# Score products in twos over two pairs of PSUM banks, and new hand-written orders, in a four-layer batch pipeline on one core

## What is computed

```
# L0: per-batch bottleneck weights from a hypernetwork
down = relu(x @ (Wd + dWd[b]).T + bd);  x = x + down @ (Wu + dWu[b]).T + bu
# L1: layer norm, weight and bias, plus a conditional bias
x = (layernorm(x) * weight + bias + tanh(lin(cond))) * weight + bias
# L2: attention block with conditional scale and shift, 16 heads of 16
h = layernorm(x) * g1 + b1;  q, k, v = split(h @ W_qkv.T + b_qkv)
o = softmax(q @ k.T / 4) @ v;  x = x + (o @ W_o.T + b_o) * a1
h = layernorm(x) * g2 + b2;  x = x + (gelu_tanh(h @ W_f1.T + b_f1) @ W_f2.T + b_f2) * a2
# L3: RMS norm, gated unit with exact gelu, 8-bit rows, ternary weights
h = x * scale(cond) * rsqrt(mean(x*x) + eps);  val, gate = split(h @ up_w.T)
y = quant8(val * gelu(gate)) @ ternary(down_w).T;  out = y + x
```

## Time and profile before

| | before |
|---|---|
| median of 3 runs | 934.47 us |
| span of the profiled execution | 933.9 us |
| PE busy | 843.1 us (90%), 5852 instructions |
| VectorE (DVE) busy | 565.4 us (61%) |
| ScalarE (ACT) busy | 510.9 us (55%) |
| GpSimd (POOL) busy | 231.2 us (25%) |

### The profile page before, as it was taken

One profiled execution on the slowest core, in us unless ns is written; L12 is line 12 of the kernel. 1 busy time (PEld: TensorE's weight loads), 2 busy tenths in 40 slices (PEclk: granted clock), 3 DMA queues, 4 the chain that ended last, 5 costly groups with the idle time before them and its releaser, 6 DMA issues.

```text
span 933.9 us, 15916 instructions
## 1 busy us (share of the span) xinstructions
PE 843.1 (90%) x5852; PEld 633.5 (68%) x5852; DVE 565.4 (61%) x1063; ACT 510.9 (55%) x796; POOL 231.2 (25%) x333
## 2 busy tenths in 40 slices
PE   6642577999999999999999999999999999999977
PEld 4101355687777778787878787878777777776665
DVE  1212586575757667575858585858485867656424
ACT  1101444565565657574748575656666574756542
POOL 1001204150405041323232231405050514130310
PEclk9855777999999999999999999999999999999998
DMA  9997643423161433324151515151424132320000
GB/s 344 365 366 252 248 138 124 148 80 122 62 203 38 135 97 114 120 78 156 47 187 47 188 47 188 46 173 61 154 76 142 65 127 80 104 80 25 24 12 12
DMA packets 58477, 118.48 MB, mean 127 GB/s; under 512 B 6336, under 2 KB 15936, under 8 KB 55696
## 3 DMA queue, kind: packets, MB, share of 16 engines
q1 hardware_dynamic: 58400, 117.48, 36.6%
...
## 4 chain that ended last, share of the span: by engine, by line
PE 74%; issue 9%; DMA 7%; DVE 4%; ACT 2%; SPq 2%; POOL 2%; POOLq 0%; DVEq 0%; ACTq 0%
PE bank L486 30%; PE bank L692 11%; PE pair_s L653 6%; PE pair_s L618 5%; PE pair_t L639 5%; PE pair_t L486 4%; DMA hyp<-in_hyper 3%; PE bank L737 3%; PE bank L664 3%; PE bank L567 2%; PE bank L729 1%; PE bank L561 1%; DVE oq L1145 1%; DMA wc<-in_cols 1%; PE bank L574 1%
## 5 line engine op out<-in xcount | busy, mean ns | idle before, releaser
L851 ACT ACTIVATE Pr<-pair_t 128x1024 f32<-128x1024 f32 x128 | 131.3, 1026 | 125.2 <-PE pair_t L639 121.5
L1121 DVE TENSOR_REDUCE nmax<-pair_s 128x4 f32<-128x1024 f32 x128 | 155.8, 1217 | 34.5 <-PE pair_s L618 33.9
L692 PE MATMUL bank<-wf,G 128*128 128x256 f32 x512 | 123.0, 387 | 0.1
L486 PE MATMUL bank<-wup_hi,hD_hi 128*128 128x512 f32 x256 | 109.4, 427 | 4.8 <-POOL hD_lo L1316 4.1
L1344 POOL TENSOR_TENSOR x<-x,xcr 128x512 f32<-128x512 f32 x16 | 20.5, 1281 | 358.1 <-DVE x L1179 358.1
L692 PEld LDWEIGHTS bank<-wf,G 128*128 128x128 f32 x512 | 93.3, 190 | 15.5 <-issue 0.2
L486 PE MATMUL bank<-wup_lo,hD_hi 128*128 128x512 f32 x256 | 102.0, 398 | 0.0
L486 PE MATMUL bank<-wup_hi,hD_lo 128*128 128x512 f32 x256 | 101.9, 398 | 0.0
L618 PE MATMUL pair_s<-Kp,Qp 64*128 64x256 f32 x512 | 66.1, 337 | 21.7 <-DVE nmax L1121 13.0
L895 ACT ACTIVATE gl<-bank,rsD 128x512 f32<-128x512 f32 x64 | 44.1, 689 | 63.6 <-PE bank L486 63.4
L1189 DVE SCALAR_TENSOR_TENSOR hd<-bank,rsD,gl 128x512 f32<-128x512 f32 x64 | 47.9, 748 | 46.2 <-PE bank L486 34.7
(11 more groups left out here) (177 smaller groups left out, 1879.5 us busy)
## 6 DMA issues: line engine op xcount, KB each, us to landing
hyp<-in_hyper SPq DMA_DIRECT2D x16, 1024.0 KB, 10.2
...
```

The lines of the kernel that those rows point to most:

```text
L486: mm = pe.matmul(dst, l, r, start=first and i == 0, stop=last and i == 2)
L692: mm = pe.matmul(bank[5][:, r * D:(r + 1) * D], G[:, k, r * P:(r + 1) * P], wf2[:, k, :], start=k == 0, stop=k == FT - 1)
L851: act.activation(Pr[:, p % 4, :, :].rearrange("p a n -> p (a n)"), pair_t[:, :, :].rearrange("p a n -> p (a n)"), ACT.Exp, scale=DH ** -0. ...
L1121: dve.tensor_reduce(nmax[:, n % 2, :, p % GP, :], pair_s[:, :, :].rearrange("p a (r n) -> p a r n", r=RT), AX.X, ALU.max, negate=True).the ...
```

## The change

Seven things change. The arithmetic, the tiles and the number of matmuls stay.

1. `b_s(n)` and `b_t(n)` now issue two pairs of heads in one go, the even one into `pair_s`, the odd one into `pair_t`; both score products and both the maximum and the exponential use both pairs of banks. A pair waits for the reader of the pair two before it instead of one.
2. `b_o(n)` issues two groups in one go, so `B.o0` and `B.o1` are left of `B.o0` to `B.o3` on PE.
3. New waits go with it: the first pair of `b_t` waits for the second transposed maximum (bank 0), pair 4 of `b_t` for the transposition of bank 1, pair 5 of `b_s` for a gelu of C (banks 2 and 3), and `c_f(1)` for the maximum of pair 3.
4. The orders of all engines are new. FIRST, LAST go from 5, 14 to 6, 13, and a step of FULL may name the turn before it or behind it, so an operation can stand behind the first ones of the next turn.
5. On SyncE, storing q and k waits until the previous batch's heads are loaded (`previous_loaded`).
6. The waits for weights on PE move from entries of the list into the operation that needs them.
7. In HEAD, `W.late` (the loads of the second feed-forward weight and of the down weight) is the first entry of SyncE's turn 0, and ScalarE does `A.down` ahead of `W.qkv`.

```diff
-FIRST, LAST = 5, NB - 2
+FIRST, LAST = 6, 13
...
     "PE": """
-        B.s0 A.down C.proj B.s1 A.up D.u0 B.s2 D.u1 C.ht B.s3 D.u2 C.f0 B.m0 C.f1 C.f2 B.s4 A.ht C.f3 B.s5 D.u3 B.t0 B.s6 A.q D.qt0 B.s7 B.t1 A.k D.y0
-        B.t2 B.m1 B.o0 B.t3 C.g0 B.t4 B.o1 A.v B.t5 D.qt1 C.g1 C.g2 B.t6 C.g3 B.t7 D.y1 B.o2 B.o3 C.xt""",
+        -1: B.m1 A.v B.t0 C.g0 B.t1 C.g1 D.qt1 B.o0 C.g2 B.t2 C.g3 B.t3 D.y1 B.o1 C.xt 0: A.down B.s0 C.proj D.u0 A.up D.u1 C.ht B.s1 D.u2 C.f0 C.f1
+        C.f2 B.m0 A.ht C.f3 B.s2 D.u3 B.s3 A.q D.qt0 A.k D.y0""",
...
+    for step, text in ((0, HEAD), *((n, FULL) for n in range(FIRST, LAST)), (0, TAIL)):
+        for name in text[engine].split():
+            if name[-1] == ":":
+                t = step + int(name[:-1])
+            else:
+                order.append((t, name))
...
+        pair = [pair_s, pair_t]
...
+            def previous_loaded(a):
+                if a:
+                    for j in range(4):
+                        sp.wait_ge(heads_in[j], 32 * a)
...
+                def b_s(n):
+                    pe.wait_ge(heads_in[n], 32 * b + 32)
+                    for p in (2 * n, 2 * n + 1):
+                        if p == 0:
+                            past(pe, dve_o, DVE_O, "tr1", b, 1)
+                        elif p == 1:
+                            past(pe, act_t, ACT_T, f"exp{NP - 1}", b, 1)
+                        elif p == GP:
+                            pe.wait_ge(dve_m, at(DVE_M, "t0", b))
+                        elif p == GP + 1 and with_c:
+                            pe.wait_ge(act_c, at(ACT_C, "gelu5", c))
+                        else:
+                            pe.wait_ge(dve_s, at(DVE_S, f"max{p - 2}", b))
...
+                                mm = pe.matmul(pair[p % 2][:, half, r * L:(r + 1) * L], Qp[lo:lo + KR, 1 - par, p, r * P:(r + 1) * P],
+                                               Kp[lo:lo + KR, 1 - par, p, :], start=True, stop=True)
...
+                def b_t(n):
+                    if n % 2 == 0:
+                        pe.wait_ge(mx_in[n // 2], 32 * b + 32)
+                    for p in (2 * n, 2 * n + 1):
+                        if p == 0:
+                            pe.wait_ge(dve_m, at(DVE_M, f"t{NG - 1}", b))
+                        elif p == GP:
+                            pe.wait_ge(dve_o, at(DVE_O, "tr0", b))
+                        elif p > 1:
+                            pe.wait_ge(act_t, at(ACT_T, f"exp{p - 2}", b))
...
+                def b_o(n):
+                    if n == 0:
                         pe.wait_ge(act_a, at(ACT_A, "v", b))
-                        pe.wait_ge(dve_s, at(DVE_S, f"max{NP - 1}", b))
-                    if g == 2:
-                        pe.wait_ge(dve_o, at(DVE_O, "tr0", b))
-                    pe.wait_ge(act_t, at(ACT_T, f"exp{2 * g + 1}", b))
+                    for g in (2 * n, 2 * n + 1):
+                        pe.wait_ge(act_t, at(ACT_T, f"exp{GP * n + 2 + g % 2}", b))
...
                 def c_f(n):
...
+                    if n == 1 and t <= NB:
+                        pe.wait_ge(dve_s, at(DVE_S, f"max{GP - 1}", b))
```

More of the change, by code:

```diff
@@ L77 @@
     "PE": """
[L78 to L81, removed]
@@ L99 @@
+        A.ln A.ht C.g3 C.xt""",
 }
@@ L145, in sequence @@
     out = []
-    full = [x for t in range(FIRST, LAST) for x in (f"{t}:", *FULL[engine].split())]
-    t = 0
-    for name in (*HEAD[engine].split(), *full, *TAIL[engine].split()):
-        if name[-1] == ":":
-            t = int(name[:-1])
-            continue
+    order, t = [], 0
+    for step, text in ((0, HEAD), *((n, FULL) for n in range(FIRST, LAST)), (0, TAIL)):
[4 more added lines that the diff above has]
+                order.append((t, name))
+    for t, name in order:
         what = name[2:].rstrip("0123456789")
@@ L577, in a_q @@
                 def a_q():
+                    if a == 0:
+                        pe.wait_ge(dve_w, at(DVE_W, "qkv", 0))
                     pe.wait_ge(pool_a, at(POOL_A, "lo", a))
@@ L643, in b_o @@
-                def b_o(g):
-                    if g == 0:
-                        pe.wait_ge(act_a, at(ACT_A, "v", b))
-                        pe.wait_ge(dve_s, at(DVE_S, f"max{NP - 1}", b))
-                    if g == 2:
-                        pe.wait_ge(dve_o, at(DVE_O, "tr0", b))
-                    pe.wait_ge(act_t, at(ACT_T, f"exp{2 * g + 1}", b))
-                    for k in range(RT):
-                        for j in range(4):
-                            mm = pe.matmul(bank[1][32 * j:32 * j + 32, (g % 2) * L:(g % 2 + 1) * L], Va[:, 1 - par, k, 4 * g + j, :],
-                                           Pr[:, (2 * g + j // 2) % 4, j % 2, k * L:(k + 1) * L], start=k == 0, stop=k == RT - 1)
-                    mm.then_inc(pe_o, 1)
+                def b_t(n):
[8 more added lines that the diff above has]
+                            pe.wait_ge(act_t, at(ACT_T, f"exp{p - 2}", b))
+                        for k in range(RT):
+                            for half in range(2):
+                                lo = 64 * half
+                                mm = pe.matmul(pair[p % 2][:, half, k * L:(k + 1) * L], Kp[lo:lo + KR, 1 - par, p, k * P:(k + 1) * P],
+                                               Qp[lo:lo + KR, 1 - par, p, :], start=True, stop=True)
+                        mm.then_inc(pe_t, 1)
@@ new lines, in b_o @@
+                def b_o(n):
+                    if n == 0:
+                        pe.wait_ge(act_a, at(ACT_A, "v", b))
+                    for g in (2 * n, 2 * n + 1):
+                        pe.wait_ge(act_t, at(ACT_T, f"exp{GP * n + 2 + g % 2}", b))
+                        for k in range(RT):
+                            for j in range(4):
+                                mm = pe.matmul(bank[1][32 * j:32 * j + 32, (g % 2) * L:(g % 2 + 1) * L], Va[:, 1 - par, k, 4 * g + j, :],
+                                               Pr[:, (2 * g + j // 2) % 4, j % 2, k * L:(k + 1) * L], start=k == 0, stop=k == RT - 1)
+                        mm.then_inc(pe_o, 1)
@@ L741, in turn @@
                     if stage == "W":
-                        {"qkv": with_qkv, "fa": with_f1, "up": with_up, "abs": mean_size}[what]()
+                        mean_size()
                     elif stage == "A" and what in ("down", "up", "ht", "q", "k", "v"):
```

149 lines of the change are left out of this document (66 added, 83 removed).

## The result

The changed kernel takes 892.24 us, the median of four runs (889.3 to 892.63), beside 934.74 for the kernel before (four runs, 932.58 to 937.58). The ratio is 0.954, with an interval of 0.9517 to 0.9563. The forecast was 897.0, in a range of 886 to 911. So the total came out near it; the parts did not, as the profile shows. It is of an execution with a span of 890.8 us.

The account below looks back on a forecast made before the run. PE, busy 90% of the span, was taken as the bound. The terms -26.0 - 3.5 - 8 - 1.5 + 1.5 = -37.5 on 933.9 gave 896.4, and 897 us with 0.6 between span and median; range 886 to 911.

Parts of the forecast that it names:

- The price of a change of form: PE, turns 3 to 15: switching between 128-row and smaller products costs 0.185 us; eleven fewer save 2.0 per turn, -26.0 in all.
- +1.5: PE, the turns in the middle: new waits, chiefly c_f(1) for the maximum of pair 3, cost 0.1 us per turn.
- -8: Head, the start of the span: fewer waits for maxima and an earlier relu gain 8 us, bounds 0 and -13.
- turn 2's -2.0: PE, turn 2: from 29 to 18 changes of form at 0.185 us, part of -3.5 for turns 2 and 16.
- the maximum sets the pace: Turn 1: with two pairs of banks VectorE's 1.22 us maximum paces the score products, gaining up to 7 x 1.0 us.
- 7 less 2 given back: Turn 1: up to 7 us gained on waits for maxima, 2 given back for VectorE's split of the up weight.
- Turn 0 gave its share: Turn 0: ScalarE's relu goes ahead of the qkv weight copy, for which PE waited 3.64 us; taken as -1.
- Rival 3: Turns 1 and 2: denser work also brings the full clock sooner, so the head gains more; 888 us or less, chance 0.08.
- The 2 us given back for the up weight's split: Head, VectorE: the 4.40 us split stands ahead of the transposition that pair 4 of the second product awaits; +2.
- ScalarE's 12 table loads: ScalarE: 12 more loads at 1.28 us, 15 us more on an engine with room, covered; no cost.
- SyncE: Store queue: previous_loaded waits for loads issued a whole stretch of the turn earlier; costs nothing, with 3 us to spare.
- Tail: -1.5: Turn 17: feed-forward products fill PE's waits of 1.12 us for copied transposes and 0.67 for an output row; -1.5.

Follow-up runs that it names:

- e11: The kernel before with 85 unused matmuls added on PE where it stood idle in turns 0 to 2: 932.4 us, ratio 0.9981.
- The four runs on the clock: Unused matmuls added in PE's idle time: changed kernel with head filled 887.27 us, tail 888.72, both 883.26; kernel before with turns 0 to 2 filled 932.4.

## Why the prediction was right or wrong

**The price of a change of form: right.** The forecast had 2.0 us per turn from eleven changes fewer, and the traces have just these eleven (31 and 20 per turn; a small transposition between wide products adds nothing to the distances, so it is not counted). The measured turn is 2.42 shorter (49.12 to 46.70). A turn before without its wait is 48.78, so 2.1 are left for the changes of form, 0.19 each. The split twos had 0.16 to 0.19 per change; by the lower price 0.3 of the 2.1 stay without a cause.

**New waits: wrong, and the step that failed is "+1.5".** The forecast let the 0.3 us of the first score product go against a new wait of 0.2 at the projection, and added 0.1 per turn for `c_f(1)` and the like. Neither wait came. The projection's operand came 0.05 us ahead of it. The maximum of pair 3 was ready 13.3 us after the projection and PE came at 13.8, where the forecast had 14.1 and 14.2. The whole of the old wait, 0.34, was gained; together with the forecast's new waits this makes about 0.45 us per turn, 4.5 of the 5.3 us by which the ten turns from 5 to 14 did better (24.2 measured, 18.9 by the sum).

**Turns 3, 4, 15 and 16: a term that was missing.** They gained 3.7, 3.9, 3.4 and 3.6 us, together 14.6, where the sum had 1.9, 1.9, 1.9 and 1.4. Four causes can be read from the traces. The forecast counted 41 changes of form fewer in these turns, and there are 44 (65 to 40 in turns 3 and 4, 57 to 38 in 15 and 16). PE's waits fell from 2.7 to 0.9 in turns 3 and 4 (before: 1.0 for the rows of maxima, 0.8 for GpSimd, 0.3 each for the transposition of bank 1, an exponential and a load) and from 4.1 to 2.6 in turns 15 and 16 (before: 1.4 for the projection's operand, 1.4 for maxima, 0.7 for a sum that GpSimd makes, and smaller ones). And the two products that went over into the head are somewhat over 1 us. In turn 16 the kernel before also had 3.4 us of busy time at the half level of the clock (853.5 to 856.9), which the changed kernel has not; in the profile of e11, where it did not come either, the same turn took 45.2 us and not 46.3. With 44 changes at 0.185 these make some 13.8 of the 14.6. I had read waits there for turn 17 alone and priced turns 3 to 16 by one turn in the middle. Part of this is scatter: turn 4 of the kernel before took 51.0, 49.6 and 50.0 us in three profiles. These four turns and the ten before make the 12.8 us by which the middle did better.

**The head: wrong in size, -8 and turn 2's -2.0 against -3.5.** The terms make -10, and the text's place for the projection, 177, -9. The mechanism came as described: the waits for maxima fell from 13.0 to 2.7, more than the forecast's 5. But the time went elsewhere. In turn 1 of the kernel before, the half level of the clock lay for the most part over PE's waits, where it cost next to nothing. In the changed kernel it lay over the value products of turn 1, 3.19 and 3.64 us for 32 where they take 1.9. In turn 2 both had it over the first feed-forward products (0.54 in 147 to 154 us of the changed kernel, 0.50 in 146.9 to 157.1 of the one before), so there it tells them apart little. The step that failed is "the maximum sets the pace": it does for two twos, and then PE at the half level does. The four runs on the clock show it: turn 1 so filled is 6.4 to 7.8 us shorter than that of the kernel before so filled, some 2 of it moved work, where the sum had 7 less 2 given back, and the head 10 to 12 us, of which up to 3 may be the half level left in turn 2 of the latter. Turn 0 gave its share: `A.up` starts at 76.05 us, not 78.19, of which 0.7 us is left at `a_ht`; in the other profiles of the changed order it starts at 73.6 to 75.1, so the scatter ahead of it is as large as this term. A further 1 us of the 6.5 is no loss but the two products that the head now carries. Rival 3 had the clock wrong: denser work did not bring the full clock sooner by itself. Both kernels had 30.7 us at the half level between 100 and 160 us, and a second profile of the changed one 27.3.

**The 2 us given back for the up weight's split: wrong.** The split ran at 121.51 us for 4.40 and was done before the values of turn 1 were; the transposition behind it waited for PE's value products. The term should have been 0. The two megabytes ahead of the next batch's weights took 18.6 us to land where they took 9.0, and cost nothing either.

**ScalarE's 12 table loads: right at nothing.** In the earlier trace rows the gelu starts 1.30 us after its load began, and the run with 12 loads fewer differs from the changed kernel by 0.3 us inside ranges of 2. The Trainium skill, ScalarE: Activation LUTs, What ACT_TABLE_LOAD costs, adds a drain of 1.38 us to each switch; by it the forecast's estimate was 1 us more. The trace has no room for such a drain, and the times are too close to tell 1 us.

**SyncE: right at nothing.** No wait of PE on loads appears between turns 3 and 16. `previous_loaded` was not taken out in a run, so that rests on the profile alone.

**Tail: -1.5, measured -0.9**, of which no run tells more; the wait for `oT` ahead of turn 17's projection went from 0.7 to 1.5 us.

The errors of the middle (12.8 us too little) and of the head (6.5 too much) were of opposite sign, and with 0.6 from the tail they leave 5.7 us by the rounded parts: the span's 890.8 against 896.4. The total was closer than its parts deserved, and that is luck.
